# Relative-position products of a windowed attention block: eight fills in the score buffers, or four in the attention output's two banks

## The chip, the core and the metric

One NeuronCore of a Trainium2 chip runs the whole program. The metric is device microseconds of one execution. TensorE is PE here, its weight loads PEld, VectorE DVE, ScalarE ACT, GpSimd POOL, and SP is the engine that issues most DMAs.

## What is computed

Eight images of 32x32 tokens with 96 channels go through two attention layers and a mixture of four experts. Layer 0 normalizes by groups and has a relative-position term:

```python
attn = jnp.einsum('bqd,bkd->bqk', q * SCALE, k)
rel_h = jnp.einsum('bhwc,hkc->bhwk', r_q, Rh)
rel_w = jnp.einsum('bhwc,wkc->bhwk', r_q, Rw)
attn = attn + rel_h[:, :, :, :, None] + rel_w[:, :, :, None, :]
out = softmax(attn) @ v            # 6 heads of 16
x = x + out @ proj_w + proj_b
t = t + causal_attention(layernorm(t))             # layer 1
t = t + sum_e gate_e * (gelu(layernorm(t) @ w1_e + b1_e) @ w2_e + b2_e)    # 4 experts, top 2
```

`rel_h` and `rel_w` are what the change is about: for each of the 32 rows r of an image a product with a window of the row table (32 results for 6 heads x 32 queries = 192 columns), and for each of its 32 columns one with the column table. That is 64 small products for each image.

## The kernel before

The eight images are pipelined by hand. Each engine has its own program, written out in order and joined by semaphores; nothing reorders it. One turn of the loop runs the attention of layer 1 for image i (`attention(it, 1)`), then the attention of layer 0 for image i+1 (`attention(it, 0)`), and then the **mix** (`mix(it)`), in which three parts are interleaved: the values and relative products of layer 0 for the image after the next ("rel"), the experts of image i ("a"), and the way from layer 0's output to layer 1's operands of image i+1 ("next_mix"). The order in the mix is the hand-written list `MIX`, and every engine walks through it and does its own share of each entry. Of the eight turns, the first six have all three parts, the seventh has no "rel", and the eighth has the experts alone. Ahead of them is a prologue, with the first image's relative products in a stage of its own (`p_rel`), the first image's attention of layer 0, and a first mix that has "rel" and "next_mix" but no experts. So the relative products are made eight times: in the prologue, in the first mix, and in six mixes with experts. The mixes are counted from that first one: the second to the seventh mix are those six.

PSUM has three tensors: `psT` (two slots of two banks each), which every fill of the mix takes in turn, `psS` (two banks) for row maxima and for the experts' second product, and `psOM` (two banks): `psO` holds the attention output while an attention runs, and `psM` the transposed maxima and the gate's scores. In the mix `psOM` is used for the gate's scores, and then for the transposed outputs of the experts (`back`).

A **fill** of relative products is `bias` on PE: for each of four rows r it writes two products of 192 columns, the row one (L551) into partitions 0 to 31 and the column one (L553) into partitions 32 to 63 of a `psT` slot. The column one reads its queries with a stride of 32 elements. There are eight fills for an image. For each, ACT's `rel` copies the row part and the column part (L993, L994; 32 partitions x 768) as bf16 into `qa`, and DVE's `rel` subtracts each copy from the same PSUM values and writes the rest into `qb` (L1341). DVE's second subtraction frees the slot. PE takes a slot again when the fill before the last has left it.

Six of the eight fills stand at the head of the mix, behind the two fills of layer 0's values (`val0`, L540). The seventh and the eighth stand among the experts. The other entries that matter: `ln` is ACT's logarithm and exponential of the softmax denominators (`den`, L982 and L984), which waits for the DMAs of layer 0's output; `gate` is the gate's scores on PE (L723) and a chain of small operations on DVE and ACT (L1286 and L1287, L1025, to L1306); `den` is DVE's share of the denominators (L1231, L1232, L1234), which writes `att`; `res` is the output projection on PE (L707) with the residual and the norm's statistics on DVE (L1246 to L1267); `nrm` is the rest of the norm (L879 and L881 on ACT, L1167 to L1273 on DVE); `up` and `down` are the experts' two products (L731, L745), with the gelu on ACT (L1010) between; `back` is the transposition of an expert's output (L762) from `yt`, which ACT writes (L1018).

## Time and profile before

| | |
|---|---|
| median of 3 runs | 2269.95 us (2269.05 to 2271.08) |
| the profiled execution | 2265.12 us |
| its span in the trace | 2263.3 us, mean granted clock 0.9 |
| PE | 1939.9 us busy, 86% of the span |
| DVE | 1257.3 us, 56% |
| ACT | 1099.7 us, 49% |
| POOL | 141.6 us, 6% |
| the fills' matmuls L551 and L553 | 256 each (64 fills of 4 and 4) |
| L993 and L994, mean of one | 797 and 799 ns |
| L1341, mean of one | 948 ns |

The shares are means over very different stretches. In the attentions PE, ACT and DVE take turns; in the mix the experts keep PE occupied, and the fills at its head occupy all three. The trace's timeline gives for each engine what ran, in order, and behind it in brackets how long the engine had been idle and what ended that.

### The profile page before, as it was taken

What the parts mean: (1) busy time and instruction counts of PE and PEld (TensorE: products, weight loads), DVE (VectorE), ACT (ScalarE), POOL (GpSimd) and SP (SyncE); (2) the same over time, 40 slices, a digit from 0 to 9 for tenths busy, and PEclk for the clock granted to TensorE, in tenths of its full rate; (3) what the DMA queues carried; (4) which work ended last, traced back from release to release, by engine and by line L of the source; (5) the groups of instructions that cost most, each with busy time, mean ns of one, the idle gap of its engine ahead of it and who ended that gap; (6) DMA issues with size and microseconds to landing.
All of it is one profiled execution on the core that took longest, in us unless ns stands there. A gap on an engine that the chain in (4) does not pass through costs nothing.

```text
span 2263.3 us, 28980 instructions
## 1 busy us (share of the span) xinstructions
PE 1939.9 (86%) x9408; PEld 782.6 (35%) x9408; DVE 1257.3 (56%) x2512; ACT 1099.7 (49%) x1408; POOL 141.6 (6%) x68
## 2 busy tenths in 40 slices
PE   0389579998899988999899988999889988998849
PEld 0123223343333433344333433334333433343324
DVE  5374567554664557644775557645675546744521
ACT  0326434663456634664356634565346644554323
POOL 0000001100010000200010000200002000100010
PEclk9579679988999889989899889998899898999778
DMA  1703430253005230253003430061302530001100
GB/s 43 140 1 86 68 61 18 51 90 77 8 19 107 30 79 19 51 94 63 21 18 80 61 79 11 25 114 38 57 20 48 94 70 6 19 12 45 32 10 7
DMA packets 55741, 111.45 MB, mean 49 GB/s; under 512 B 17686, under 2 KB 18903, under 8 KB 54040
## 3 DMA queue, kind: packets, MB, share of 16 engines
q1 hardware_dynamic: 54040, 109.06, 25.5%
q8 instruction: 90, 1.47, 0.3%
q14 instruction: 75, 0.61, 0.1%
q10 hardware_dynamic: 1536, 0.30, 0.1%
HBM read 61.82 MB, written 34.60 MB: 43 GB/s over the span
## 4 chain that ended last, share of the span: by engine, by line
issue 60%; PE 22%; DVE 6%; POOL 4%; DMA 3%; SPq 2%; ACT 2%; POOLq 0%; DVEq 0%; ACTq 0%
PE psOM L621 5%; PE psS L566 4%; DVE mx L1220 3%; PE psT L598 2%; PE psT L599 2%; PE psS L745 2%; PE psT L731 2%; POOL split L1088 1%; PE psT L601 1%; PE psT L531 1%; SPq L397 1%; DMA scr<-split 1%; PE psT L775 1%; DMA kb<-scr 1%; POOL lb L1097 1%
## 5 line engine op out<-in xcount | busy, mean ns | idle before, releaser
L954 ACT ACTIVATE probs<-psT 128x1024 f32<-128x1024 f32 (+7 forms) x768 | 622.2, 837 | 532.4 <-PE psT L599 265.7
L1220 DVE TENSOR_REDUCE mx<-psS 128x1 f32<-128x512 f32 (+3 forms) x1152 | 704.8, 643 | 304.3 <-PE psS L566 226.2
L599 PE MATMUL psT<-qb,kb 97*128 97x512 f32 x768 | 416.0, 586 | 0.0
L621 PE MATMUL psOM<-probs,v 128*32 128x512 f32 (+3 forms) x2688 | 385.3, 559 | 12.0 <-ACT probs L954 12.0
L566 PE MATMUL psS<-ka,qa 128*128 128x512 bf16 x768 | 299.2, 400 | 32.0 <-DVE mx L1220 20.6
L598 PE MATMUL psT<-qa,ka 128*128 128x512 bf16 x768 | 297.0, 387 | 15.7 <-DMA qb<-negr 7.4
L731 PE MATMUL psT<-xf,w1s 97*128 97x512 f32 x384 | 206.6, 669 | 1.6 <-DVE mrow L1314 1.6
L1341 DVE TENSOR_TENSOR qb<-psT,qa 32x768 fp32r<-32x768 f32 x128 | 121.3, 948 | 150.7 <-ACT qa L993 149.0
L745 PE MATMUL psS<-probs,w2s 128*96 128x512 f32 x384 | 189.8, 618 | 6.3 <-ACT probs L1010 6.3
L1010 ACT ACTIVATE probs<-psT 128x1024 f32<-128x1024 f32 x96 | 98.1, 1023 | 196.2 <-PE psT L731 196.0
L601 PE MATMUL psT<-qr,kr 97*128 97x512 bf16 (+3 forms) x576 | 185.7, 349 | 2.8 <-DMA qr<-negb 1.0
L566 PEld LDWEIGHTS psS<-ka,qa 128*128 128x128 bf16 x768 | 71.7, 98 | 304.1 <-DVE mx L1220 262.7
L599 PEld LDWEIGHTS psT<-qb,kb 97*128 97x128 f32 x768 | 151.2, 197 | 44.4 <-issue 1.4
L566 PE MATMUL psS<-kr,qr 96*128 96x512 bf16 (+3 forms) x384 | 138.8, 374 | 17.6 <-DVE mx L1220 12.3
L1314 DVE TENSOR_REDUCE mrow<-psT 128x1 f32<-128x128 f32 (+7 forms) x128 | 92.9, 755 | 83.8 <-PE psT L778 83.8
L598 PEld LDWEIGHTS psT<-qa,ka 128*128 128x128 bf16 x768 | 76.3, 99 | 148.7 <-issue 84.8
L775 PE MATMUL psT<-kr,qr 96*128 96x512 bf16 (+1 forms) x192 | 68.1, 437 | 57.0 <-DMA kr<-scr 30.4
L621 PEld LDWEIGHTS psOM<-probs,v 128*32 128x32 f32 x2688 | 67.6, 108 | 126.1 <-issue 83.0
L731 PEld LDWEIGHTS psT<-xf,w1s 97*128 97x128 f32 x384 | 77.8, 212 | 92.2 <-issue 79.1
L1088 POOL TENSOR_TENSOR split<-resid,split 96x1024 bf16<-96x1024 f32 x16 | 34.1, 2129 | 1110.3 <-ACT split L912 1110.3
L1323 DVE SCALAR_TENSOR_TENSOR x<-psOM,g,x 128x96 f32<-128x96 f32 x256 | 60.4, 307 | 69.3 <-PE psOM L762 69.1
L745 PEld LDWEIGHTS psS<-probs,w2s 128*96 128x96 f32 x384 | 62.3, 170 | 98.8 <-issue 94.2
(140 smaller groups left out, 1732.2 us busy)
## 6 DMA issues: line engine op xcount, KB each, us to landing
scr<-split SPq DMA_DIRECT2D x32, 576.0 KB, 4.2
scr<-qb SPq DMA_DIRECT2D x16, 768.0 KB, 6.7
qr<-scr SPq DMA_DIRECT2D x48, 192.0 KB, 6.6
au<-ot SPq DMA_DIRECT2D x192, 32.0 KB, 2.0
lb<-ot SPq DMA_DIRECT2D x192, 32.0 KB, 2.0
qr<-scr SPq DMA_DIRECT2D x48, 128.0 KB, 4.4
kr<-scr SPq DMA_DIRECT2D x48, 128.0 KB, 7.2
qa<-scr SPq DMA_DIRECT2D x32, 128.0 KB, 3.9
```

What stands on the lines that cost most here:

```text
L566: last = mm(bank[:, 0:n], q[0:rows, h, t * P:(t + 1) * P], k[0:rows, h, kc * HALF:kc * HALF + n], start=True, stop=not diagonal)
L598: mm(o[:, a:b], ka[:, h, ks], qa[:, h, a:b], start=True, stop=False)
L599: last = mm(o[:, a:b], kb[:, h, ks], qb[:, h, a:b], start=False, stop=True)
L601: last = mm(o[:, a:b], kr[:, h, ks], qr[:, h, a:b], start=True, stop=a != q0)
L621: last = mm(psO[j:j + 2 * HD, a - c * HALF:HALF], v[:, kt, 2 * p + hh, :], probs[:, (2 * kt + hh) % 4, a:(c + 1) * HALF], start=kt == 0, s ...
L731: last = mm(o[:, c * HALF:(c + 1) * HALF], w1s[:, a:a + P], xf[:, c * HALF:(c + 1) * HALF], start=True, stop=True)
L745: last = mm(psS[0:C, c, :], w2s[:, n, :], hbuf[:, n % 4, c * HALF:(c + 1) * HALF], start=j == 0, stop=j == HJ - 1)
L954: A(probs[:, n % 4, q0:T], psT[:, t_slot(ts, m), q0:T], ACT.Exp).then_inc(t_free, 1)
L1010: A(hbuf[:, n % 4, :], psT[:, t_slot(stage, fill), :], ACT.Gelu).then_inc(ta_free, 1)
L1220: V.reduce_max(mx[layer][:, p % 2, (h % 2) * NT + t, kc:kc + 1], psS[:, s_bank(st, fill), 0:max_cols(layer, t, kc)], AX).then_inc(s_free, 1)
L1314: V.reduce_max(mrow[:, 0, n:n + 1], psT[:, t_slot(st, fill), 0:cols], AX).then_inc(t_free, 1)
L1341: ins = V.tensor_tensor(rest[0], rest[1], lead[0], ALU.subtract)
```

## The change

The relative products leave `psT`. They are now made in four fills of sixteen products, each of which takes both banks of `psOM`: for each i, the row and column products of row 8g+i in partitions 0 to 63, and those of row 8g+4+i in partitions 64 to 127. So four products stand side by side in the four groups of 32 partitions. A fill has semaphores of its own: `rel_full` when PE has made all sixteen, and `rel_free` when DVE has made its four subtractions. PE waits for `rel_free` of the fill before ahead of each fill, since there is one buffer in place of two slots. ACT makes four copies for a fill and DVE four subtractions, in the shapes of before.

All four fills stand at the head of the mix, and none stands among the experts. The gate's scores, which are written to `psM`, wait until the last fill is free. ACT loads its table of exponentials explicitly at `ln`. The experts' outputs alternate between `xg` and `att` in place of `xg` alone, and ACT's wait ahead of them is for one `back` less.

```diff
-REL_FILLS = HS // REL_STEP
+REL_FILLS = HS // (2 * REL_STEP)
...
-MIX = ([("val0", 0), ("val0", 1)] + [("rel", g) for g in range(6)]
-       + [("ln", 0), ("gate", 0), ("up", 0), ("up", 1), ("den", 0), ("down", 0), ("up", 2), ("rel", 6), ("down", 1), ("res", 0),
-          ("up", 3), ("down", 2), ("rel", 7), ("up", 4), ("down", 3), ("nrm", 0), ("back", 0), ("up", 5), ("down", 4),
+MIX = ([("val0", 0), ("val0", 1)] + [("rel", g) for g in range(4)]
+       + [("ln", 0), ("gate", 0), ("up", 0), ("up", 1), ("den", 0), ("down", 0), ("up", 2), ("down", 1), ("res", 0),
+          ("up", 3), ("down", 2), ("up", 4), ("down", 3), ("nrm", 0), ("back", 0), ("up", 5), ("down", 4),
...
-        yt = xg[0:C, :]
+        yts = (xg[0:C, :], att[0:C, :])
...
-            def bias(o, g):
+            def bias(it, stage, g):
+                pe.wait_ge(rel_free, upto("rel_free", it, stage, g))
+                o = psOM[:, :, :].rearrange("p b f -> p (b f)")
                 q_cols = qr[0:C, :, :].rearrange("c h (a b) -> c h a b", b=WS)
                 for i in range(REL_STEP):
-                    r = REL_STEP * g + i
-                    window = slice(HS - 1 - r, 2 * HS - 1 - r)
-                    mm(o[0:HS, 256 * i:256 * i + NH * WS], relt[:, 0, window], qr[0:C, :, r * WS:(r + 1) * WS],
-                       start=True, stop=True)
-                    last = mm(o[HS:2 * HS, 256 * i:256 * i + NH * HS], relt[:, 1, window], q_cols[:, :, :, r],
-                              start=True, stop=True)
-                last.then_inc(t_full, 1)
+                    for u in range(2):
+                        r = REL_STEP * (2 * g + u) + i
+                        window = slice(HS - 1 - r, 2 * HS - 1 - r)
+                        j = 2 * HS * u
+                        mm(o[j:j + HS, 256 * i:256 * i + NH * WS], relt[:, 0, window], qr[0:C, :, r * WS:(r + 1) * WS],
+                           start=True, stop=True)
+                        last = mm(o[j + HS:j + 2 * HS, 256 * i:256 * i + NH * HS], relt[:, 1, window],
+                                  q_cols[:, :, :, r], start=True, stop=True)
+                last.then_inc(rel_full, 1)
...
             def gate_scores(it):
                 pe.wait_ge(s_free, upto("s_free", it, "mix", 0))
                 pe.wait_ge(m_free, upto("m_free", it, "mix", 0))
+                pe.wait_ge(rel_free, upto("rel_free", it, "mix", incs("rel_free", "mix", kind_of(it))))
...
-                act.wait_ge(t_full, upto("t_full", it, stage, fill + 1))
-                rows, cols = rel_views(qa, 64, g, psT[:, t_slot(stage, fill), :])
-                A(rows[0], rows[1], ACT.Copy).then_inc(rel_lead, 1)
-                A(cols[0], cols[1], ACT.Copy).then_inc(rel_lead, 1)
+                act.wait_ge(rel_full, upto("rel_full", it, stage, g + 1))
+                for u in range(2):
+                    rows, cols = rel_views(qa, 64, g, u)
+                    A(rows[0], rows[1], ACT.Copy).then_inc(rel_lead, 1)
+                    A(cols[0], cols[1], ACT.Copy).then_inc(rel_lead, 1)
...
-                act.wait_ge(y_full, upto("y_full", it, stage, i))
+                act.wait_ge(y_full, upto("y_full", it, stage, max(i - 1, 0)))
...
                     elif what == "ln":
+                        exp_table()
                         den(it, "mix")
...
+                for u in range(2):
+                    views = zip(rel_views(qa, 64, g, u), rel_views(qb, 0, g, u))
+                    for i, (lead, rest) in enumerate(views):
+                        dve.wait_ge(rel_lead, upto("rel_lead", it, stage, 4 * g + 2 * u + i + 1))
+                        ins = V.tensor_tensor(rest[0], rest[1], lead[0], ALU.subtract)
+                ins.then_inc(rel_free, 1)
```

PE at the head of a mix with experts, before: the last of the six fills and the gate's scores. What a row waits for stands in brackets.

```order
L551 MATMUL psT<-qr,relt 32x192 [waits t_free]
L553 MATMUL psT<-qr,relt 32x192
...
L720 REGISTER_ALU
L721 REGISTER_ALU [waits s_free]
L723 MATMUL psOM<-gw,xf 128x4 [waits m_free]
```

And of the change, the last of the four fills (its two rows stand eight times) and the gate's scores:

```order
L555 MATMUL psOM<-qr,relt 32x192 [waits rel_free]
L557 MATMUL psOM<-qr,relt 32x192
...
L724 REGISTER_ALU
L726 REGISTER_ALU [waits m_free,s_free]
L728 MATMUL psOM<-gw,xf 128x4 [waits rel_free]
```

Each fill and the gate's scores now wait for the fill just ahead; before, a fill waited for the last but one, and the gate's scores for none.

PE between the third `up` and the output projection in such a mix, before:

```order
L731 MATMUL psT<-xf,w1s 128x512 [waits ta_free]
...
L551 MATMUL psT<-qr,relt 32x192 [waits ta_free]
L553 MATMUL psT<-qr,relt 32x192
...
L745 MATMUL psS<-probs,w2s 96x512 [waits ta_free]
L745 MATMUL psS<-probs,w2s 96x512
L522 REGISTER_ALU [waits att_ready]
L707 MATMUL psT<-wp0,att 128x96 [waits ta_free]
```

And of the change:

```order
L738 MATMUL psT<-xf,w1s 128x512 [waits ta_free]
L738 MATMUL psT<-xf,w1s 128x512
L750 REGISTER_ALU
L752 MATMUL psS<-probs,w2s 96x512 [waits ta_free]
L752 MATMUL psS<-probs,w2s 96x512
L711 MATMUL psT<-wp0,att 128x96 [waits ta_free,att_ready]
```

The seventh fill is gone from its place; the eighth stood five entries later, between the third `down` and the fifth `up`, and is gone in the same way.

## Rows read from the trace of the kernel before

**Rows 1.** timeline, PE, fourth mix: start us, us, engine, line, tiles, [idle <-releaser]

```profile
994.72 0.26 PE L551 MATMUL psT<-qr,relt 96*32 96x192 bf16 x1
...
999.01 0.34 PE L551 MATMUL psT<-qr,relt 96*32 96x192 bf16 x1 [1.54 <-DVE qb L1341]
...
1003.30 0.34 PE L551 MATMUL psT<-qr,relt 96*32 96x192 bf16 x1 [0.90 <-DVE qb L1341]
...
1006.64 3.58 PE L723 MATMUL psOM<-gw,xf 97*128 97x4 f32 x16
```

**Rows 2.** timeline, ACT and DVE over the same fills and just behind

```profile
1000.51 0.80 ACT L993 ACTIVATE qa<-psT 32x768 bf16<-32x768 f32 x1 [1.02 <-PE psT L553]
...
1001.34 3.85 DVE L1341 TENSOR_TENSOR qb<-psT,qa 32x768 fp32r<-32x768 f32 x4 [0.44 <-ACT qa L993]
...
1008.39 1.06 ACT L982 ACTIVATE il<-lb 96x1024 f32<-96x1024 f32 x1
...
1010.70 0.23 ACT L1025 ACTIVATE g<-g 128x32 f32<-128x32 f32 x1 [0.17 <-DVE g L1287]
```

**Rows 3.** windows: stretch, us, busy of each engine, PEclk, DMA share, GB/s

```profile
1006.60:1015.30 8.70, 8.70 (x23) 5.60 (x23) 7.05 (x19) 6.24 (x7) 0.00 (x0) 0.50 0.09 11
1006.60:1062.00 55.40, 55.40 (x189) 27.67 (x188) 29.55 (x80) 32.11 (x38) 2.12 (x1) 0.92 0.13 34
```

**Rows 4.** timeline, PE, the eighth fill of the fourth mix, and a weight load

```profile
1028.23 0.26 PE L551 MATMUL psT<-qr,relt 96*32 96x192 bf16 x1
1028.23 0.48 PE L553 MATMUL psT<-qr,relt 96*32 96x192 bf16 x1
1028.33 0.41 PE L551 MATMUL psT<-qr,relt 96*32 96x192 bf16 x3
1028.54 1.15 PE L553 MATMUL psT<-qr,relt 96*32 96x192 bf16 x3
...
1028.54 0.11 PEld L553 LDWEIGHTS psT<-qr,relt 96*32 96x32 bf16 x1
```

**Rows 5.** timeline, PE: products in four column groups, and across the whole array

```profile
980.78 1.06 PE L621 MATMUL psOM<-probs,v 128*32 128x512 f32 x8
...
1031.44 1.88 PE L745 MATMUL psS<-probs,w2s 128*96 128x512 f32 x4
```

**Rows 6.** timeline, PE and DVE, around the seventh and eighth fill

```profile
1016.87 1.22 DVE L1234 SCALAR_TENSOR_TENSOR att<-il,au 96x1024 f32<-96x1024 f32 x1
...
1019.73 0.26 PE L551 MATMUL psT<-qr,relt 96*32 96x192 bf16 x1
...
1021.12 1.96 PE L745 MATMUL psS<-probs,w2s 128*96 128x512 f32 x4
1022.91 1.92 PE L707 MATMUL psT<-wp,att 97*128 97x96 f32 x16
...
1029.62 1.98 PE L731 MATMUL psT<-xf,w1s 97*128 97x512 f32 x4
```

**Rows 7.** timeline, ACT and DVE, the first mix (no experts)

```profile
246.69 1.06 ACT L982 ACTIVATE il<-lb 96x1024 f32<-96x1024 f32 x1
...
259.45 1.28 ACT L884 ACT_TABLE_LOAD   x1
...
260.99 0.21 ACT L881 ACTIVATE sm<-sm 128x8 f32<-128x8 f32 x1
...
248.87 1.22 DVE L1231 TENSOR_TENSOR lb<-lb,il 96x1024 f32<-96x1024 f32 x1 [1.08 <-ACT il L984]
...
259.95 1.91 DVE L1341 TENSOR_TENSOR qb<-psT,qa 32x768 fp32r<-32x768 f32 x2
```

**Rows 8.** timeline, ACT and DVE, the prologue

```profile
86.44 0.80 ACT L993 ACTIVATE qa<-psT 32x768 bf16<-32x768 f32 x1 [15.11 <-DMA scr<-qb]
...
104.03 1.28 DVE L1178 BATCH_NORM_STATS2 gs<-xg 96x6 f32<-96x512 f32 x2
...
112.56 0.69 DVE L1220 TENSOR_REDUCE mx<-psS 128x1 f32<-128x512 f32 x1 [3.32 <-PE psS L566]
```

More of the change, by code:

```diff
@@ L107, in fills @@
 def fills(stage, kind):
-    return [x for x in steps(stage, kind) if x[0] in ("up", "rel", "max", "res", "tr", "qk", "val", "val0")]
+    return [x for x in steps(stage, kind) if x[0] in ("up", "max", "res", "tr", "qk", "val", "val0")]
 def by_act(what):
@@ L761, in back @@
                 for t in range(NT):
-                    last = mm(psOM[:, t // 4, (t % 4) * C:(t % 4 + 1) * C], yt[:, t * P:(t + 1) * P],
+                    last = mm(psOM[:, t // 4, (t % 4) * C:(t % 4 + 1) * C], yts[x % 2][:, t * P:(t + 1) * P],
                               ident[0:C, 0:C], is_transpose=True, start=True, stop=True)
@@ L790, in mix @@
                             pe.wait_ge(qr_in, upto("qr_in", it, "mix", 0))
-                        bias(take_mixed(it, "mix", (what, n)), n)
+                            pe.wait_ge(o_free, upto("o_free", it, "mix", 0))
+                            pe.wait_ge(m_free, upto("m_free", it, "mix", 0))
+                        bias(it, "mix", n)
                     elif what == "up":
@@ L860, in _, with rel_views @@
             mix(B - 1)
-        def rel_views(dst, base, g, o):
-            o = o.rearrange("p (i r) -> p i r", r=256)[:, :, 0:NH * HS]
-            r = slice(REL_STEP * g, REL_STEP * (g + 1))
+        def rel_views(dst, base, g, u):
+            j = 2 * HS * u
+            o = psOM[j:j + 2 * HS, :, :].rearrange("p b (i r) -> p (b i) r", r=256)[:, :, 0:NH * HS]
+            r = slice(REL_STEP * (2 * g + u), REL_STEP * (2 * g + u + 1))
             return ((dst[base:base + HS].rearrange("p h (a b) -> p a h b", b=WS)[:, r],
@@ L984, in den, with rel @@
                 A(il[:, :], il[:, :], ACT.Exp, scale=-1.0).then_inc(il0, 1)
-            def rel(it, stage, g, fill):
+            def rel(it, stage, g):
                 if g == 0:
@@ L1014, in expert_out @@
                 i = x
[L1015 removed]
+                act.wait_ge(y_full, upto("y_full", it, stage, max(i - 1, 0)))
                 for c in range(NC):
                     act.wait_ge(s_full, upto("s_full", it, stage, 2 * i + c + 1))
[L1018 removed]
+                    A(yts[x % 2][:, c * HALF:(c + 1) * HALF], psS[0:C, c, :], ACT.Identity,
                       bias=b2s[:, x:x + 1]).then_inc(s_free, 1)
@@ L1028, in mix @@
                     elif what == "rel":
-                        rel(it, "mix", n, fills("mix", kind_of(it)).index((what, n)))
+                        rel(it, "mix", n)
                     elif what == "up":
@@ L1333, in norm, with rel @@
                     V.tensor_copy(xf[0:C, b * HALF:(b + 1) * HALF], psS[0:C, b, :]).then_inc(s_free, 1)
-            def rel(it, stage, g, fill):
-                o = psT[:, t_slot(stage, fill), :]
-                views = zip(rel_views(qa, 64, g, o), rel_views(qb, 0, g, o))
-                for i, (lead, rest) in enumerate(views):
-                    dve.wait_ge(rel_lead, upto("rel_lead", it, stage, 2 * g + i + 1))
-                    ins = V.tensor_tensor(rest[0], rest[1], lead[0], ALU.subtract)
-                ins.then_inc(t_free, 1)
+            def rel(it, stage, g):
+                for u in range(2):
[4 more added lines that the diff above has]
+                ins.then_inc(rel_free, 1)
             def mix(it):
@@ L1350, in mix @@
                     elif what == "rel":
-                        rel(it, st, n, fills(st, kind_of(it)).index((what, n)))
+                        rel(it, st, n)
                     elif what == "back":
```

22 lines of the change are left out of this document (12 added, 10 removed).

## The prediction

> **What bounds the kernel now.** I read the timeline of one mix first, engine by engine, and the page's shares only after it, since they mix attentions and mixes. The mix near 993 us stands for the six with experts. PE begins the first fill at 994.72 us and the gate's scores at 1006.64 [rows 1]: the six fills at the head take 11.92 us. There the reader is to see what ends PE's waits: DVE's subtraction L1341, since two slots go round. From 999.01 to 1003.30 is one round of two fills, 4.29 us. In it DVE subtracts for 3.85 us with a pause of 0.44 [rows 2], so DVE is almost the bound. From 1006.64 on PE is the bound: in the window from 1006.60 to 1062.00 it is busy for all of 55.40 us [rows 3]. So whatever delays the gate's scores delays everything behind it one for one, and whatever leaves PE's row of work there comes back one for one.
>
> **A fill of the change, step by step.** One fill of eight products lasts from 1028.23 to 1028.54 + 1.15 = 1029.69, 1.46 us [rows 4]. Inside it the three later column products take 1.15 us, so with one product's own 0.5 us they start 0.32 us apart. The three later row products take 0.41 us together and run beneath them, in the other column group. At half clock it is no longer: from PE's start at 999.01 [rows 1] to ACT's first copy at 1000.51 [rows 2] pass 1.50 us. So the column products set the length, by the rate at which their strided queries come, not by the array.
>
> The new fill has two such pairs side by side. The trace doesn't show two strided streams at once. The lower bound is 1.50 us to the first copy, if the four groups run as one. The upper bound is eight column products in a row: 1.50 + 4 x 0.32 = 2.78. I take the lower end, because its nearest row is of the same form: the eight records of L621, in four column groups with different moving data, take 1.06 us, where four records across the whole array take 1.88 [rows 5]; four streams side by side cost there as much as one.
>
> Then come one copy before DVE can start (1000.51 to 1001.34, 0.83 us) and four subtractions in a row (3.85 us [rows 2]). They are in the shapes of before and go at the same price. DVE's last subtraction frees the fill, and PE follows some 0.04 later. One fill is 1.50 + 0.83 + 3.85 + 0.04 = **6.22 us**, with nothing of the next under it, because each fill takes both banks and the next waits for it. Before, PE and the first copy of one slot lay under the subtractions of the other.
>
> **A mix with experts (six times).** Four fills are 24.88 us against 11.92: the gate's scores start **12.96 later**. They wait for the last fill, and behind them stand the experts and the way to layer 1. The seventh and the eighth fill leave PE's busy stretch: 1019.73 to 1021.12 and 1028.23 to 1029.62 [rows 4, 6], 1.39 each, **2.78 back**. Can that really come back? The output projection L707 would start at 1021.52 on the old clock, and `att` is ready at 1016.87 + 1.22 = 1018.09 [rows 6]: yes, by 3.4 us. DVE and ACT lose two subtractions and two copies for each removed fill there, which makes their own waits shorter. Net 12.96 - 2.78 = 10.18, six times **61.1 us**.
>
> ACT's added table load at `ln` costs nothing here. ACT's last copy of the last fill ends 1.50 + 4 x 0.83 = 4.8 us after the fill's start, 1.4 ahead of the gate's scores. With the load (1.28 [rows 7]) and the logarithm and exponential (2.18, from 246.69 to 248.87 [rows 7]) it is free 2.1 after the gate's start. The gate's exponential is wanted only at 1010.70 - 1006.64 = 4.1 after it [rows 1, 2]. If that cover were gone the price would be 1.28 in each. In the seventh mix ACT waits for the denominators' DMAs in any case, so the load is hidden there. The second buffer `att` for the experts' outputs and the looser wait ahead of them cost and bring nothing: each `back` stands in the list ahead of the next expert's last `down`.
>
> PE's clock is granted at half (1.2 GHz) for 8.70 us from the gate on [rows 3]. The thinner head can't take it below that level. It can move the return by a microsecond or so either way, at half of that in time: up to 0.75 us in each of six, which I take as 0 and keep at 5 us for the range.
>
> **The first mix.** It has no experts to give anything back, and its way is that of the denominators. Before, from PE's first fill to L982 pass 1008.39 - 994.72 = 13.67 us [rows 1, 2]; the first mix has the same head. Of the change, L982 comes after three whole fills, the fourth's 1.50, four copies and the table load, which is in the way here: 18.66 + 1.50 + 3.32 + 1.28 = 24.76. That is 11.1 later. The eighth fill is gone from the way: DVE's subtractions of it (259.95, 1.91 us) end at 261.86 and only then does the norm go on, while ACT, held up by that fill's copies and a table load, ended at 261.20. Without it ACT's two small steps follow the statistics at once and are done near 260.4 [rows 7]: 1.45 back. Net **9.65 us**.
>
> **The prologue.** The first copy waits for DMAs until 86.44 and DVE is done with the fills at 104.03 [rows 8]. Of the change it is done at 86.44 + 0.83 + 3.85 + 3 x 6.22 = 109.8, 5.8 later. But DVE then stood idle for 3.32 us ahead of the first row maxima, waiting for PE and its DMAs at 112.56 [rows 8], and this absorbs as much: **2.45 us**.
>
> **Sum.** 61.1 + 9.65 + 2.45 = 73.2 us. The profiled execution took 2265.12 us, so 2338.3. The median of the runs is 4.8 above it, 2269.95: the forecast is **2343 us**. Its own range, with the clock's 5 us and a little for the fill's start, is 2334 to 2353.
>
> **Rivals.** (1) The two column products of a pair share the rate at which strided data come, so the fill is not four side by side in effect. Each fill is then 1.28 longer, in 28 fills of the mixes and in 3 of the prologue (its first starts long before ACT's DMA wait ends): 31 x 1.28 = 40 us, 2383 us. For it speaks that the column product is four times slower than the row one (0.32 against 0.08 apart) at either clock, so that something outside the array limits it. Against it speak the row products, which run beneath a column product without slowing it [rows 4], and L621.
>
> (2) Side by side, but paced by the weight loads: sixteen loads of 0.11 us [rows 4] in a row are 1.8 us, to which the last product adds its 0.3: some 2.0 to the copy, 0.5 more for each of 31 fills, 15 us, 2358 us. Against it: L621's eight records need eight loads too, and take 1.06 us [rows 5]. The Trainium skill points to something between: its page "TensorE: Matmul & The Clock Gate", section "Measured speedup vs the span model", gives 2.38 for three column tiles, not 3. By that an estimate of the fill is 1.46 x 3 / 2.38 = 1.84 us and of the time 2355 us; L621's row doesn't agree, with four groups at the price of one.
>
> (3) Not slower. The point from which the head costs nothing is a fill of (11.92 + 2.78) / 4 = 3.68 us. That needs copies and subtractions of about 0.42 us in place of 0.8 and 0.96. The mechanism would be that ACT and DVE slowed each other in one slot's banks and no longer do when they read different partitions of `psOM`. At 0.40 each a fill is 3.54, a mix with experts gains 0.5, and the whole is near 2268 us with the prologue and the first mix at no cost. Against it: L993 (797 ns), which starts while DVE may be idle, and L994 (799 ns), which runs beside a subtraction, take the same.
>
> **Chances.** The forecast 0.60, rival 1 0.20, rival 2 and what lies between 0.14, rival 3 0.02, something else 0.04. The range has to take in the first three: 2334 to 2386. A measurement of this kernel can tell 0.2%, 4.5 us, from no change; faster 0.01, within it 0.02, slower 0.97.
>
> **What would show it.** In the profile after, PE's fills in a mix start 6.2 us apart with a wait of some 4.7 on DVE ahead of each; the gate's scores start 24.9 after the first fill; DVE pauses about 2.4 between groups of four subtractions. Rival 1 shows column products 0.16 apart on average over sixteen products becoming 0.32, and 2.8 from PE's start to the first copy; rival 2 shows 2.0. Output projection and experts stand behind the gate's scores as before, less 1.39 and 2.78. I am wrong in the sum if PE has new waits between the gate and the last `down`, or if the clock comes back later than 10 us after the gate.

## The result, and the profile after

The change takes 2348.52 us (median of 4 runs, 2345.11 to 2350.66) against 2270.51 for the kernel before on the same chip (4 runs, 2269.05 to 2274.01): a ratio of 1.0339 [1.0326, 1.0352], slower by 78.0 us. The forecast was +73.2 and 2343. The profiled execution took 2350.66 us, its span is 2348.9 us and its mean granted clock 0.88; before these were 2265.12, 2263.3 and 0.90.

First the page of the kernel after: the busy time of each engine, and of the groups the subtraction and the row products. Behind the last bar stand the idle time of the engine just ahead of that group and what ended most of it.

```profile
PE 1896.0 (81%) x9314; PEld 771.1 (33%) x9408; DVE 1257.1 (54%) x2512; ACT 1110.2 (47%) x1416; POOL 141.6 (6%) x68
...
L1353 DVE TENSOR_TENSOR qb<-psOM,qa 32x768 fp32r<-32x768 f32 x128 | 121.8, 952 | 162.6 <-ACT qa L1004 161.3
...
L555 PE MATMUL psOM<-qr,relt 96*32 96x192 bf16 x256 | 24.3, 336 | 135.3 <-DVE qb L1353 116.9
```

DVE's busy time is what it was (1257.3 before), and ACT's is 10.5 more, which is the eight table loads of 1.28 us. PE's is 43.9 less, and that is the fills: side by side, their products keep PE busy for 48.1 us where it was 92.1 before. (The trace after also lacks 94 of PE's 9408 records, all in two groups of the attentions, L570 and L602; PE's busy time outside the fills is all but the same, 1848.4 for 1850.4.) So no engine has more work to do apart from the table loads; the time is in waits. The L555 group alone shows 135 us of PE idle ahead of the fills, 117 of it ended by DVE's subtraction.

Next the timeline after, PE and ACT and DVE over the second fill of the fourth mix and the start of the third (start, us, engine, line, in brackets the idle time and its releaser). It answers to [rows 1, 2].

```profile
1037.34 0.34 PE L555 MATMUL psOM<-qr,relt 96*32 96x192 bf16 x1 [4.78 <-DVE qb L1353]
1037.34 0.49 PE L557 MATMUL psOM<-qr,relt 96*32 96x192 bf16 x1
1037.35 0.34 PE L555 MATMUL psOM<-qr,relt 96*32 96x192 bf16 x1
1037.35 0.49 PE L557 MATMUL psOM<-qr,relt 96*32 96x192 bf16 x1
...
1038.00 0.83 PE L557 MATMUL psOM<-qr,relt 96*32 96x192 bf16 x4
...
1038.87 0.80 ACT L1004 ACTIVATE qa<-psOM 32x768 bf16<-32x768 f32 x1 [2.99 <-PE psOM L557]
1039.70 3.85 DVE L1353 TENSOR_TENSOR qb<-psOM,qa 32x768 fp32r<-32x768 f32 x4 [2.42 <-ACT qa L1004]
1043.61 0.34 PE L555 MATMUL psOM<-qr,relt 96*32 96x192 bf16 x1 [4.78 <-DVE qb L1353]
...
1056.12 3.58 PE L728 MATMUL psOM<-gw,xf 97*128 97x4 f32 x16 [4.78 <-DVE qb L1353]
```

Read it as a relay: PE 1037.34 to the copy at 1038.87 (1.53), one copy until 1039.70 (0.83), four subtractions until 1043.55 (3.85), PE again at 1043.61 (0.06). The period is 6.27 us, and in it each engine stands still while the other two have their turn: PE 4.78, DVE 2.42, ACT 2.99. Nothing overlaps but three of ACT's four copies with DVE. The gate's scores start at 1056.12, 25.02 after the first fill at 1031.10.

The two column products of a pair, rows and columns of two different groups of four rows, start within the same hundredth of a microsecond (1037.34 and 1037.35), and each is as long as a column product of before (0.49 against 0.48 [rows 4]). The last four of them take 0.83 together: two pairs 0.32 apart, and the last one's 0.5.

The windows after (us, then busy time of PE, PEld, DVE, ACT and POOL, PEclk, DMA share, GB/s): the head of the fourth mix, and the fifth mix from the gate to the end of its row maxima, counted to PE's last product for them. The third row is the same stage of the fifth mix before. In the fifth mix PE has 17 products fewer after: the 16 of the two fills that left, and one that the window before cuts at its edge.

```profile
1031.10:1056.10 25.00, 5.90 (x65) 2.27 (x64) 15.23 (x16) 14.70 (x19) 0.00 (x0) 0.60 0.55 72
...
1332.50:1409.30 76.80, 70.34 (x232) 33.75 (x232) 35.10 (x96) 29.59 (x35) 2.13 (x1) 0.86 0.28 57
```

```profile
1269.20:1345.30 76.10, 69.91 (x249) 33.59 (x248) 41.87 (x103) 34.50 (x41) 2.12 (x1) 0.90 0.29 60
```

In the head PE is busy for 5.90 of 25.00 us. From the gate on, the stage after has two fills less in it and yet isn't shorter in this mix: 76.80 against 76.10. PE is busy for as long as before, 70.34 us against 69.91, with less to do, and its granted clock is 0.86 against 0.90. The prediction took that clock as unchanged. What a microsecond at half clock costs in this stage is read further down, from mixes that differ in it.

The whole difference between the two spans, stage by stage (us; sums over the trace; half clock is the time at the granted level of 1.2 GHz):

| stage | before | after | difference | forecast |
|---|---|---|---|---|
| start to the first mix's first fill | 232.9 | 236.0 | +3.1 | +2.45 |
| first mix, to the end of its row maxima | 70.7 | 79.8 | +9.1 | +9.65 |
| six mixes: head, first fill to gate | 71.6 | 151.0 | +79.4 | +77.8 |
| six mixes: gate to the end of the row maxima | 467.4 | 456.8 | -10.6 | -16.7 |
| (half clock in that stage) | 109.1 | 125.8 | +16.7 | 0 |
| seventh mix, from the gate | 81.1 | 81.1 | 0 | 0 |
| attentions | 1282.9 | 1287.6 | +4.7 | 0 |
| the rest | 56.7 | 56.6 | 0 | 0 |
| span | 2263.3 | 2348.9 | +85.6 | +73.2 |

### The profile page after: what moved, and what is told of

It reads as the page before. It is cut to its first block, busy times and chain, and to the rows that moved or that the text cites. A ratio compares the mean times of both kernels' runs of the same rounds, so it can differ in the third digit from the quotient of the medians.

```text
span 2348.9 us, 28871 instructions
## 1 busy us (share of the span) xinstructions
PE 1896.0 (81%) x9314; PEld 771.1 (33%) x9408; DVE 1257.1 (54%) x2512; ACT 1110.2 (47%) x1416; POOL 141.6 (6%) x68
## 4 chain that ended last, share of the span: by engine, by line
issue 61%; PE 21%; DVE 7%; POOL 4%; DMA 3%; ACT 2%; SPq 1%; POOLq 0%; DVEq 0%; ACTq 0%
PE psOM L625 4%; PE psS L570 4%; DVE mx L1232 3%; PE psT L603 2%; PE psT L602 2%; PE psS L752 2%; PE psT L738 2%; POOL split L1100 1%; PE psT L605 1%; DVE qb L1353 1%; PE psT L532 1%; SPq L398 1%; DMA scr<-split 1%; PE psT L782 1%; POOL lb L1109 1%
## 5 line engine op out<-in xcount | busy, mean ns | idle before, releaser
L570 PE MATMUL psS<-ka,qa 128*128 128x512 bf16 x722 | 283.5, 402 | 22.2 <-DVE mx L1232 14.5
L602 PE MATMUL psT<-qa,ka 128*128 128x512 bf16 x720 | 279.5, 388 | 11.3 <-DVE resid L1221 4.0
L1353 DVE TENSOR_TENSOR qb<-psOM,qa 32x768 fp32r<-32x768 f32 x128 | 121.8, 952 | 162.6 <-ACT qa L1004 161.3
L570 PEld LDWEIGHTS psS<-ka,qa 128*128 128x128 bf16 x768 | 72.0, 98 | 301.0 <-DVE mx L1232 263.7
L570 PE MATMUL psS<-kr,qr 96*128 96x512 bf16 (+3 forms) x384 | 139.2, 375 | 17.6 <-DVE mx L1232 12.3
L555 PE MATMUL psOM<-qr,relt 96*32 96x192 bf16 x256 | 24.3, 336 | 135.3 <-DVE qb L1353 116.9
L602 PEld LDWEIGHTS psT<-qa,ka 128*128 128x128 bf16 x768 | 76.5, 100 | 149.2 <-issue 84.7
```

What stands on the lines that cost most here:

```text
L570: last = mm(bank[:, 0:n], q[0:rows, h, t * P:(t + 1) * P], k[0:rows, h, kc * HALF:kc * HALF + n], start=True, stop=not diagonal)
L602: mm(o[:, a:b], ka[:, h, ks], qa[:, h, a:b], start=True, stop=False)
L1353: ins = V.tensor_tensor(rest[0], rest[1], lead[0], ALU.subtract)
```

## The experiments

Each ratio is to runs of the kernel before on the same chip. Two buffers, narrow fills, the order of products and the first spread list share one set of those (median 2268.54 us), the two kernels on the table load and the second spread list another (2268.99), and the last spread list has its own (2271.15).

### Two buffers again, all else wide

Two things of the change lengthen the head: a fill of sixteen products, and one buffer in place of two. Here the sixteen-product fills go into the two slots of `psT`, so two are in flight. The list is that of the change, four fills at the head; the table load and the second `yt` are left out.

```diff
-                pe.wait_ge(rel_free, upto("rel_free", it, stage, g))
-                o = psOM[:, :, :].rearrange("p b f -> p (b f)")
...
-                        bias(it, "mix", n)
+                        bias(take_mixed(it, "mix", (what, n)), n)
```

> The kernel before with one part of the change alone: four fills of sixteen products, four side by side, all ahead of the experts, but in the two psT slots, so that two fills are in flight. No added table load, gate's scores don't wait for the last fill. Theory S (the loss is the single buffer: product, first copy and four subtractions in a row, nothing of the next fill under them): DVE subtracts nearly without a pause, 16 x 0.96 us; the third fill starts 6.2 us after the first and the fourth 10.1, the gate's scores 11.6 after the first fill (before 11.9), the seventh and eighth fill are gone from PE's busy stretch (2.8 us each mix): about 3 us less in each of six mixes, first mix and prologue unchanged: 2251 us (2243 to 2259). Rival W (four products side by side, or having all of them ahead, is what costs): as slow as the change, 2335 to 2350. Rival T (the table load costs in each mix): 2340.

Measured: 2253.34 us (5 runs), ratio 0.9932 [0.9909, 0.9956] to before, 2 us above what was expected. The fourth mix in its timeline, PE and DVE, first fill to gate:

```profile
993.62 0.26 PE L553 MATMUL psT<-qr,relt 96*32 96x192 bf16 x1
...
999.87 0.34 PE L553 MATMUL psT<-qr,relt 96*32 96x192 bf16 x1 [3.49 <-DVE qb L1346]
...
1003.75 0.34 PE L553 MATMUL psT<-qr,relt 96*32 96x192 bf16 x1 [2.38 <-DVE qb L1346]
...
1005.16 3.58 PE L725 MATMUL psOM<-gw,xf 97*128 97x4 f32 x16
```

```profile
995.97 15.48 DVE L1346 TENSOR_TENSOR qb<-psT,qa 32x768 fp32r<-32x768 f32 x16 [7.43 <-ACT qa L997]
```

Sixteen subtractions now run in one row of 15.48 us, 0.97 each and without a pause, where the change needs four rows of 3.85 with 2.4 between. PE still waits for DVE, but a fill ahead. Beside the change, the head falls from 25.0 to 11.54 us and the whole from 2348.5 to 2253.3. So the loss isn't in the wide fill, nor in putting all of them at the head: it is in the one buffer. The wide fill is even worth something. All 64 products stand ahead of the gate in 11.54 us, where six eighths of them took 11.92 [rows 1]. Two smaller parts of the change are absent here too: the table load, which has a run of its own below, and the second `yt`, which no run tests by itself.

### One buffer, narrow fills

If the one buffer costs one relay for each fill, then eight fills of eight products must cost more than four of sixteen, though the work is the same.

```diff
-REL_FILLS = HS // (2 * REL_STEP)
+REL_FILLS = HS // REL_STEP
...
-                    for u in range(2):
-                        r = REL_STEP * (2 * g + u) + i
+                    for u in range(1):
+                        r = REL_STEP * (g + u) + i
```

> The change with eight fills of eight products in psOM, all ahead, each waiting for the one ahead. Theory S: a fill is 1.50 + 0.83 + 1.93 + 0.06 = 4.32 us, eight are 34.6 against 25.1: 9.5 more in each of six mixes, in the first mix and in the prologue, 76 in all: 2424 us (2415 to 2433). Rival W (the side-by-side products or their sixteen in two banks cost): the narrow fills are no dearer per product, 2348 or less.

Measured: 2412.41 us (2 runs), ratio 1.0637 [1.0603, 1.0671]. Its timeline, the second and third fill of the fourth mix:

```profile
1071.50 0.34 PE L555 MATMUL psOM<-qr,relt 96*32 96x192 bf16 x1 [2.83 <-DVE qb L1353]
...
1075.79 0.34 PE L555 MATMUL psOM<-qr,relt 96*32 96x192 bf16 x1 [2.83 <-DVE qb L1353]
```

```profile
1069.53 1.91 DVE L1353 TENSOR_TENSOR qb<-psOM,qa 32x768 fp32r<-32x768 f32 x2 [7.41 <-ACT qa L1004]
1073.82 1.91 DVE L1353 TENSOR_TENSOR qb<-psOM,qa 32x768 fp32r<-32x768 f32 x2 [2.38 <-ACT qa L1004]
```

The period is 4.29 us, DVE's pause in it 2.38, as in the change (2.42). The relay's fixed part, PE's products and the first copy, is paid for each fill whether eight or sixteen products are in it, and the head is 34.33 us. This also measures the product side by itself. Sixteen products take 1.53 us from PE's start to ACT's copy at half clock; eight take 1072.99 - 1071.50 = 1.49. The second pair of column groups costs 0.04.

The time missed its expectation of 2424 (2415 to 2433) by 12 us, though the fills came as expected: against the change the six heads are 55.1 us longer, the first mix 9.7 and the prologue 10.7, 75.5 for the 76 that were put. What was left out is the stage from the gate to the end of the row maxima, the same instructions in both kernels: over six mixes it is 8.9 us shorter (448.0 for 456.8), with 22.6 us less at half clock (103.2 for 125.8). The attentions are 4.0 shorter as well.

### The order of the products in a fill

Rival 1 held that two column products side by side would share a rate. The change issues the two next to each other. Here the loop over u is outside, so that all eight products of one pair of column groups are issued ahead of the other eight.

```diff
-                for i in range(REL_STEP):
-                    for u in range(2):
+                for u in range(2):
+                    for i in range(REL_STEP):
```

> The change with the loop over u outside the loop over i: the eight products of partitions 0 to 63 come first in the program, then those of 64 to 127. Theory S: the four column groups take their products from a queue far enough ahead that the order doesn't matter: 1.5 us from PE's start to the first copy, a fill of 6.27, 2348 us. Rival O (products start in program order): the second eight start late, 2.3 to 2.8 us to the first copy, 0.8 to 1.3 more for 31 fills, 2373 to 2388.

Measured: 2342.86 us (2 runs), ratio 1.0331 [1.0298, 1.0363]; against the change's 1.0339 [1.0326, 1.0352] no difference. The second fill of the fourth mix:

```profile
1034.77 0.34 PE L555 MATMUL psOM<-qr,relt 96*32 96x192 bf16 x1 [4.81 <-DVE qb L1353]
1034.77 0.49 PE L557 MATMUL psOM<-qr,relt 96*32 96x192 bf16 x1
1034.80 0.34 PE L555 MATMUL psOM<-qr,relt 96*32 96x192 bf16 x1
1034.80 0.49 PE L557 MATMUL psOM<-qr,relt 96*32 96x192 bf16 x1
...
1035.08 0.50 PE L557 MATMUL psOM<-qr,relt 96*32 96x192 bf16 x1
...
1035.11 0.50 PE L557 MATMUL psOM<-qr,relt 96*32 96x192 bf16 x1
...
1036.33 0.80 ACT L1004 ACTIVATE qa<-psOM 32x768 bf16<-32x768 f32 x1 [3.02 <-PE psOM L557]
```

This was not what the order in the program suggests. The products of the second pair of column groups are issued ninth and later. If they started in that order, the second four column products would begin behind the first four, 0.32 apart, and the copy would come after 2.3 to 2.8 us, as the expectation's rival has it. It comes after 1.56 (1.53 in the change), and the trace has a second row and column product 0.03 us behind the first, too soon for the same group. The next column products follow in the same way, two within 0.03 us, 0.31 behind the first two. So within a fill PE starts a product of a free column group while products issued ahead of it wait for theirs. The rows don't name a product's group, so this is read from the times. Rival 1 gets nothing from it: neither form shows two column streams that slow each other.

### The table load

The change loads ACT's table explicitly at `ln`. The prediction hid it in all mixes but the first, where it put 1.28 us. Here that line is left out, and nothing else; the change itself ran again beside it.

```diff
-                        exp_table()
                         den(it, "mix")
```

> The change without the table load that it adds at ln (the denominators' logarithm then runs on the table that the attention left). Theory L (the load is in the way in the first mix alone): L992's row of the first mix starts 1.3 us earlier, the gates of the other mixes as before, 1.3 us less in all, which the runs can't tell from the change. Rival T (it is in the way in all seven mixes with relative products or in all eight): 9 to 10 us less.

> The change once more, unchanged, for the 5 us that it came out above the forecast. Theory K (they are PE's clock: where the dips to half clock fall behind the gate differs from mix to mix and from run to run): the fills of the head take 25.0 to 25.4 us again, but the time from the gate's scores to the end of the row maxima, 73.8 to 77.4 us in the first profile, comes out with another sum, and the median lies anywhere from 2342 to 2351. Rival U (something in the program that the sum missed): the same stages come out the same to a few tenths.

Measured: 2344.52 us without the load (4 runs), ratio 1.0333 [1.0313, 1.0354]; 2344.60 us for the change (4 runs), ratio 1.0325 [1.0301, 1.0349]. No difference that can be told. The load's price in the first mix, ACT in the timelines of the change and of the kernel without it:

```profile
258.96 0.80 ACT L1005 ACTIVATE qa<-psOM 32x768 bf16<-32x768 f32 x1
259.79 1.28 ACT L894 ACT_TABLE_LOAD   x1
261.08 1.06 ACT L992 ACTIVATE il<-lb 96x1024 f32<-96x1024 f32 x1
```

```profile
259.58 0.80 ACT L1005 ACTIVATE qa<-psOM 32x768 bf16<-32x768 f32 x1
260.41 1.06 ACT L992 ACTIVATE il<-lb 96x1024 f32<-96x1024 f32 x1
```

Counted from the first fill (235.96 and 236.7), the logarithm starts after 25.1 and after 23.7 us, and that first mix lasts 79.8 and 80.1 us in the change's two profiles against 78.7 here. So the load costs some 1.3 us once, as put. In the six mixes it lies in time in which ACT is idle anyway. The gate's exponential in the fourth mix, with the load and without it, shows ACT's wait for DVE shorter by just the load's 1.28:

```profile
1060.18 0.23 ACT L1036 ACTIVATE g<-g 128x32 f32<-128x32 f32 x1 [2.07 <-DVE g L1299]
```

```profile
1060.62 0.23 ACT L1036 ACTIVATE g<-g 128x32 f32<-128x32 f32 x1 [3.35 <-DVE g L1298]
```

The second run of the change matters for another reason: 2344.60 against 2348.52, the same code. The forecast of 2343 is 1.6 below the one median and 5.5 below the other.

### Fills spread among the experts

If the one buffer is bearable only where PE has other work during the 4.8 us that a fill keeps it waiting, then one fill must stand at the head and three among the experts. The gate's scores wait for the first fill alone, and the first `back` goes behind the last fill, since both need `psOM`. The table load is left out.

```diff
+MIX = ([("val0", 0), ("val0", 1), ("rel", 0), ("ln", 0), ("gate", 0), ("up", 0), ("up", 1), ("den", 0), ("down", 0),
+        ("rel", 1), ("up", 2), ("down", 1), ("res", 0), ("up", 3), ("down", 2), ("rel", 2), ("up", 4), ("down", 3), ("nrm", 0),
+        ("up", 5), ("down", 4), ("rel", 3), ("up", 6), ("tr", 0), ("down", 5), ("up", 7), ("qk", 0), ("qk", 1), ("down", 6),
+        ("val", 0), ("back", 0), ("lev", 0), ("val", 1), ("up", 8), ("down", 7), ("back", 1), ("up", 9),
+        ("down", 8), ("up", 10), ("back", 2), ("down", 9)]
```

> The change with its fills spread out, without the added table load: the first fill ahead of the denominators and the gate, the second to fourth between the experts' products, each waiting for the one ahead, and the first experts' transpositions (back 0, back 1) later, behind the last fill. Same work. Theory S: what costs is PE standing still for 4.7 us of each 6.3; with experts' products under the chain it costs PE only the 1.4 us of the fill. Head up to the first down 13.5 us against before's 23.4, two more fills later at 1.4, against before's two: some 8 to 9 less than before in each of six mixes: 2217 us (2200 to 2240). Rival Q (the copies delay the gelus and the subtractions the way to layer 1, which then ends last): 2255 to 2300.

Measured: 2247.15 us (4 runs), ratio 0.9907 [0.9873, 0.9940]. Its timeline, PE in the fourth mix, the gate's scores and the second fill:

```profile
1001.84 3.58 PE L730 MATMUL psOM<-gw,xf 97*128 97x4 f32 x16 [4.78 <-DVE qb L1357]
...
1010.97 1.88 PE L754 MATMUL psS<-probs,w2s 128*96 128x512 f32 x4
1012.78 0.26 PE L556 MATMUL psOM<-qr,relt 96*32 96x192 bf16 x1
...
1014.21 1.99 PE L740 MATMUL psT<-xf,w1s 97*128 97x512 f32 x4
```

The second fill starts without a wait, takes PE 1.43 us for sixteen products, and the `up` behind it runs at once, while copies and subtractions go on beneath. The fill costs PE its own time there and nothing more. The wait of 4.78 is left once, ahead of the gate. The head is 6.24 us in place of 25.0, and the six mixes sum to 519.4 us against 607.9 of the change and 539.1 before.

The expectation of 2217 (2200 to 2240) was too good by 30 us. It put the way from the first fill to the first `down` at 13.5 us for 23.4 before; measured in the fourth mix it is 1010.97 - 995.60 = 15.37, and before 1016.20 - 994.72 = 21.48. Against before, a mix gains 5.7 us at the head and gives 2.4 back behind the gate, where one fill more stands (1.4) and 2.4 us more pass at half clock: 3.3 in place of the 8 to 9 that were expected.

### Spread further, twice

The 4.78 us ahead of the gate can be covered as well, by two `up` between the first fill and the gate's scores. Two lists do that. Both keep the table load at `ln`, unlike the first spread list, and with two `up` ahead of the gate ACT has to load its table for the gelu once more in each mix: 49 table loads in all, for 32 in the first spread list. The first also moved everything else later: `den` and `res`, the second fill behind `nrm`, the third behind `down` 6, and the last one behind `val`, just ahead of `back` 0 and 1.

```diff
+MIX = ([("val0", 0), ("val0", 1), ("rel", 0), ("up", 0), ("up", 1), ("ln", 0), ("gate", 0), ("down", 0), ("up", 2),
+        ("down", 1), ("up", 3), ("den", 0), ("down", 2), ("up", 4), ("down", 3), ("res", 0), ("up", 5), ("nrm", 0), ("down", 4),
+        ("rel", 1), ("up", 6), ("down", 5), ("tr", 0), ("up", 7), ("down", 6), ("rel", 2), ("qk", 0), ("qk", 1),
+        ("up", 8), ("down", 7), ("val", 0), ("lev", 0), ("val", 1), ("rel", 3), ("up", 9), ("back", 0), ("back", 1),
+        ("down", 8), ("up", 10), ("back", 2), ("down", 9)]
```

> The spread order taken further: first fill, then the first two ups and the gate under its copies and subtractions; the other three fills between the experts' products, the last one after layer 1's q and k (with a wait on SP ahead of the DMAs that write the fills' queries). Two more table loads a mix. Theory S: the 4.8 us that PE stood ahead of the gate in the spread kernel (1001.84) and the 4 us that the gate and the first ups took longer at half clock go: 6 to 8 us less in each of six mixes, 2205 us (2195 to 2225). Rival Q (ACT's wait for the denominators' DMAs, which lasted until 1005.2 in the spread kernel, and the way from there to layer 1 end last): 2235 or more.

Measured: 2279.83 us (4 runs), ratio 1.0056 [1.0037, 1.0075]: 33 us slower than the first spread list, and slower than before, where 2205 (2195 to 2225) was expected. PE in its fourth mix:

```profile
1012.54 1.95 PE L732 MATMUL psOM<-gw,xf 97*128 97x4 f32 x16 [1.15 <-DVE qb L1360]
...
1040.62 1.98 PE L742 MATMUL psT<-xf,w1s 97*128 97x512 f32 x4 [1.20 <-ACT probs L1028]
...
1051.77 3.39 PE L742 MATMUL psT<-xf,w1s 97*128 97x512 f32 x4 [2.43 <-DVE resid L1228]
...
1066.73 1.54 PE L774 MATMUL psOM<-cst,xg 96*128 96x96 f32 x8 [4.45 <-DVE qb L1360]
1070.35 1.54 PE L774 MATMUL psOM<-cst,att 96*128 96x96 f32 x8 [2.08 <-DVE x L1342]
```

It did not bring what it was made for. The head works (1.15 of wait for 4.78), and the end pays for it. `back` writes into `psOM` and waits 4.45 for the last fill, of which one `up` covers too little; the next `back` waits for that one's reader, 2.08. The 2.43 belongs to the fill too: the residual L1228, which frees the buffer for `up`, stands on DVE behind the four subtractions of the fill issued just ahead of q and k (from 1046.62 for 3.85 us, the residual at 1050.49). The wait of the one buffer was moved, not removed. Mixes of 92 us on average show it (551.6 for six).

The second list keeps that head and has the order of the first spread list behind it, with the fills early enough that `back` 0 follows the last one by several entries.

```diff
+MIX = ([("val0", 0), ("val0", 1), ("rel", 0), ("up", 0), ("up", 1), ("ln", 0), ("gate", 0), ("down", 0), ("up", 2),
+        ("down", 1), ("up", 3), ("den", 0), ("rel", 1), ("down", 2), ("res", 0), ("up", 4), ("down", 3), ("rel", 2),
+        ("up", 5), ("nrm", 0), ("down", 4), ("up", 6), ("rel", 3), ("down", 5), ("tr", 0), ("up", 7), ("qk", 0), ("qk", 1),
+        ("down", 6), ("val", 0), ("back", 0), ("lev", 0), ("val", 1), ("up", 8), ("down", 7), ("back", 1), ("up", 9),
+        ("down", 8), ("up", 10), ("back", 2), ("down", 9)]
```

> The head of spread2 (first fill, two ups and the gate under its copies and subtractions) with the order of spread behind it: fills 1 to 3 each ahead of q and k, back 0 early. In spread2's fourth mix the head worked (the gate's scores took 1.95 us where they took 3.58), but PE stood 2.4 us behind q and k, and 4.5 and 2.1 us around the first back, which waited for the late fourth fill. Theory S (without those waits the head's gain stays): 4 to 6 us less than spread in each of six mixes, 2218 us (2208 to 2232). Rival Q (ACT, with two more table loads and sixteen copies among the gelus, paces the experts): 2240 to 2260, with new waits of PE on L1028-like gelu rows.

Measured: 2232.53 us (4 runs), ratio 0.9830 [0.9797, 0.9863], faster than before and than the change; 2218 (2208 to 2232) was expected. Its mean granted clock is 0.91. These are the waits of PE in its third mix, from the gate to the first row maxima:

```profile
740.88 2.26 PE L730 MATMUL psOM<-gw,xf 97*128 97x4 f32 x16 [1.15 <-DVE qb L1358]
...
770.43 1.08 PE L720 MATMUL psT<-cst,xn_tok 128*96 128x128 f32 x8 [0.37 <-DVE xn_tok L1290]
775.49 5.34 PE L533 MATMUL psT<-xnt,wqkv 96*96 96x512 f32 x8 [2.27 <-ACT xnt L1015]
...
798.30 0.23 PE L785 MATMUL psT<-kr,qr 96*128 96x128 bf16 x1 [1.64 <-DMA kr<-scr]
```

They sum to 5.4 us. The six mixes sum to 506.0 us, 33.1 less than before. It uses the change's own layout, four wide fills in the two banks of `psOM`, so what made the change slow was the place of the fills, not the layout. How much of the 15 us beyond the first spread list is the covered wait (3.6 for each of six, 22 us at most), how much is the clock, whose half-clock time from the gate on fell from 123.4 to 101.6 us, and what the added table loads cost, wasn't separated.

## Why the prediction was right, and where its terms were off

**The relay and its price.** The fill was put at 1.50 + 0.83 + 3.85 + 0.04 = 6.22 us and is 1.53 + 0.83 + 3.85 + 0.06 = 6.27 in the timeline. The head was to be 24.88 us, 12.96 more than before; it is 25.0 to 25.4, 13.2 more on average, which over six mixes is 79.4 for 77.8. That the head passes on is shown by the two-buffer kernel, which takes it away (the six heads 81.6 us shorter than in the change, the stages behind them 1.3 longer), and in the other direction by the narrow fills (55.1 longer, and 8.9 shorter behind them, where less time passes at half clock). The waits came as written: 4.78 on DVE ahead of each fill (some 4.7), 2.42 between DVE's groups (about 2.4).

**The 2.78 us that come back.** This was the small term that was off: 10.6 us over six mixes in place of 16.7. The work did leave. But the stage had 16.7 us more at half clock than before. The mixes themselves show what that costs, since it differs from one to the next. Before, three of them have 14.6 to 15.2 us at half clock and take 76.1 to 76.6 us, three have 21.0 to 22.0 and take 79.0 to 80.0. In the change one has 15.8 and takes 73.8, and five have 21.4 to 22.8 and take 76.0 to 77.4. So in both kernels each further microsecond at half clock goes with 0.4 to 0.5 us more, the somewhat longer waits of those mixes included; the narrow fills give the same, 8.9 us for 22.6. And between mixes with like time at half clock the change's stage is 2.6 to 3.3 us shorter, for the 2.78 of the prediction. So the term failed not in its 2.78 but in the sentence that took the clock's part as 0 and allowed 5 us for it: 16.7 us at 0.4 to 0.5 are an estimate of 7 to 8 us. The attentions' +4.7 come with 6.4 us more at half clock in this profile; in the second profile of the change they are +2.7, with the product loop turned round -0.5 and with two buffers -2.4. The change leaves their instructions as they were, so this is within what the same code varies by; its cause wasn't looked for.

**Where the clock's part is.** The return to 2.4 GHz comes 7.0 to 10.4 us after the gate in the six mixes of the change, against 8.7 to 10.1 before: 5.6 us earlier in sum, and in one mix alone past the 10 us that the prediction named as a sign of being wrong. What it didn't foresee is a second fall in the same stage, ahead of the one that ends every mix: at 44.5 us in sum for 20.6 before, these falls are more than the whole difference of 16.7 us at half clock. The windows of the change's fifth mix show it (columns as above): from the return on, and then the stretch that begins just behind PE's wait for `kr`, the DMA that layer 1's row maxima need.

```profile
1339.60:1387.30 47.70, 44.90 (x157) 21.85 (x155) 20.44 (x62) 23.70 (x28) 2.13 (x1) 1.00 0.18 49
1387.30:1397.50 10.20, 9.32 (x17) 3.37 (x18) 1.97 (x5) 1.02 (x1) 0.00 (x0) 0.51 1.00 122
```

The fifth mix before has no such fall; its clock is whole from the return to the end of the row of work:

```profile
1278.10:1339.60 61.50, 56.24 (x211) 26.34 (x209) 29.75 (x77) 28.25 (x34) 2.12 (x1) 1.00 0.30 58
```

The wait ahead of it, in PE's timeline of the two kernels, the change first:

```profile
1386.81 0.23 PE L782 MATMUL psT<-kr,qr 96*128 96x128 bf16 x1 [2.77 <-DMA kr<-scr]
```

```profile
1327.10 0.23 PE L775 MATMUL psT<-kr,qr 96*128 96x128 bf16 x1 [2.32 <-DMA kr<-scr]
```

In the mixes where it comes, the second fall lasts 6.8 or 10.2 us in the traces of before and after, and begins with or just behind this wait. It comes in three of the six mixes before and in five of six in each of the change's two profiles, in five with the product loop turned round, in four without the table load and in all six with two buffers. With the narrow fills it comes in four, in three of them for 3.4 us alone. In all of these but before, no fill stands among the experts, and PE comes to the wait some 55 us after the gate where it came after 58. But the first spread list, with three fills among the experts and PE at the wait after 58 to 60 us, has it in five mixes as well, behind waits of 1.7 to 2.8 us. In the profiles of before and after, the waits alone seem to divide the mixes: with a fall they are 2.61 to 3.61 us, without one 2.28 to 2.49. But the change's second profile has falls behind waits of 2.29 and 2.53 and none behind 2.39, so the wait's length doesn't decide it. In these kernels a second fall, where it comes, begins at this wait; why it comes in one mix and not in another is open. That the two fills' leaving makes it more frequent isn't shown, with a single profile of before and the spread list against it. The waits themselves sum to 16.9 us over the six mixes against 15.6 before, 1.2 more: a part of the time that the two fills gave back, PE spends at `kr`'s DMA. It is contained in the comparison of mixes above and doesn't add to the clock's part.

**The first mix** was put at +9.65, from 11.1 of delay and 1.45 back, and is +9.1; without the table load it is 78.7 for 79.8. **The prologue** was put at +2.45 and is +3.1. The first row maxima start later by 115.16 - 112.56 = 2.6:

```profile
110.02 1.28 DVE L1190 BATCH_NORM_STATS2 gs<-xg 96x6 f32<-96x512 f32 x2
```

```profile
115.16 4.07 DVE L1232 TENSOR_REDUCE mx<-psS 128x1 f32<-128x512 f32 x6
```

DVE turns to the statistics at 110.02, against 109.8 in the prediction and 104.03 before [rows 8]; 6.0 later at that place became 2.6, by the same idle time that was to absorb it.

**The table load** in the six mixes: ACT is free of the load and both functions at 1057.06 + 1.06 = 1058.12, 2.0 after the gate's start (2.1 in the prediction), and the gate's exponential then waits 2.07 for DVE. That the cover is real the kernel without the load shows by its wait of 3.35 at the same place and by its equal median.

**The rivals.** Rival 1 would have 2.8 us from PE's start to the first copy; 1.53 is what stands there, and pairs of column products start together, each 0.49 long as in a fill of before. What spoke for it in the prediction was misread in one point: the column product is four times slower than the row one (0.32 against 0.08 apart) at full clock alone. At half clock the row products of before start 0.15 to 0.16 apart, from 999.01 on, while the column ones stay at 0.32. Rival 2 would have 2.0 us to the copy. The Trainium skill's page "TensorE: Matmul & The Clock Gate", section "Measured speedup vs the span model", gives 2.38 for three column tiles, and by it the prediction's estimate of the fill was 1.84. The runs don't bear that out for this shape: sixteen products cost 0.04 more than eight. Rival 3 needed copies and subtractions at half the price; they have 0.80 and 0.95 as before. The clean test of its idea is that subtractions in `psOM` (952 ns) and in `psT` (948) are the same.

**The sum.** Profile against profile the difference is 85.6 us: 73.2 forecast, 6.1 in what the two fills gave back, 4.7 in the attentions and 1.6 in the heads; the prologue's +0.65 and the first mix's -0.55 cancel. Median against median it is 78.0 and, in the second set of runs, 75.6. The 7.6 us between 85.6 and 78.0 are where the two profiled runs lie among their fellows: before's is 5.4 under its median, the change's 2.1 above. So the medians leave 5 us to explain, the terms above account for the two profiled runs, and a part of the clock's share in them is chance of the run.

## What to carry to other kernels

One buffer between three engines turns a pipeline into a relay: its period is the sum of the stages, here 6.3 us of which DVE works 3.85, and a bigger fill only pays the fixed part less often. Before moving work into a single buffer, list what the producer can do while the buffer is away; if the list is empty, as at the head of this mix, keep two buffers, and if it isn't, as among the experts, put the fills there one at a time and the next writer of the same banks well behind the last of them. Small products that fill one or two column groups are worth trying side by side: here that halved PE's time for them, and with two buffers kept the kernel was 15 us faster than before.

## What the runs showed of the hardware beyond that

Two products with strided operands in different column groups don't slow each other: starts at 1037.34 and 1037.35, each 0.49 us long, and a fill of 16 products reaches its reader in 1.53 us against 1.49 for one of 8. By the times, products of one fill don't start in the order of the program when their column groups differ: the second pair, issued ninth and later, started 0.03 us behind the first. The kernel before shows it too: by its records the last two row products of the eighth fill start at 1028.41 and 1028.49, ahead of a column product that was issued before either and starts at 1028.54 [rows 4]. And the granted clock isn't a constant of the kernel: from the gate to the end of the row maxima the time at 1.2 GHz is 14.6 to 22.0 us in the mixes of before, 15.8 to 22.8 in those of the change's first profile and 12.3 to 19.5 in the last spread list, with the same instructions in each of a kernel's mixes.
